# First routed scores issued among the last local tile's steps, with each bank and room waited for at its first use

## The chip, the cores and the metric

One core of a Trainium2 chip. The metric is the device time of one execution in microseconds (us), median of several. TensorE is called PE, VectorE DVE, ScalarE ACT, GpSimd POOL; SP is the engine whose queue issues most DMAs.

## The reference

All tensors are fp32; x is 2 sequences of 1024 tokens, 512 wide.

```
xn  = layernorm(x)
A:  q,k,v = xn Wq+bq, xn Wk+bk, xn Wv+bv      (16 query heads, 4 key/value heads, 32 wide)
    q,k = rope(rmsnorm(q)), rope(rmsnorm(k))
    local attention: a key is seen when it is not later and at most 64 back
    out_A = attention @ Wo + bo
B:  gate = softmax(xn W_gate) over 16 heads; each token keeps its best head's k (one shared
    key) and its best head's v times the gate (one shared value)
    out_B = causal attention of all 16 heads' q over the shared k and v, full length
x + out_A + out_B
```

## The kernel before

The kernel has two stages. The **local stage** goes in 8 rounds of 256 tokens (two tiles of 128): products with the weights (banks gemm, 2 of them), layernorm and transposes (bank tp1), and for each tile the local attention: scores in four banks (win), maxima on DVE, exponentials on ACT, sums on DVE, scaling on POOL, four transposes p_t through the win banks with a copy on ACT each, values (bank av), a copy and a subtraction (attn, on ACT and DVE), twelve matmuls with Wo (project, in a gemm bank), and a DVE addition into x_res (event res_r). SP then stores these rows to the DRAM tensor `partial` (event res_stored).

The **routed stage** does B in 8 units (4 groups of 4 heads, 2 sequences). A unit u has 48 row_scores (a matmul of queries against all keys in an s_ps bank and a masked maximum on DVE), which give each query's maximum; these are turned (max_in_rows) and written into two more rows of the query operand by two small DMAs (r_row by ACT's queue, r_row_lo by SP's). Then come 36 key_scores (one matmul of 512 columns in an st_ps bank, an exponential of it on ACT into a room p_t, on POOL a causal mask for the diagonal ones and an addition for pairs), key_values and key_sums (bank od_ps), row_done (copy on ACT) and finish (transposes on PE, scaling on DVE). The maxima of unit 0 (first_max) are made during the local stage, so unit 0 has only key_scores on, and in the meantime the row_scores of unit 1 run. PSUM has 8 banks; the routed stage's s_ps (4), st_ps (3) and od_ps are the same banks as gemm, tp1, win and av. Its SBUF rooms lie over tensors of the local stage too: p_t over p_loc, p_loc_t and qkv, the pair sums over cos_t and others, the query operand q_op over the weights w_tok, out_sb[1] over x_res.

The order of all steps is written out by a planner (`make_plan`, class `Routed`) with assumed costs per engine: it emits one list of steps, and every engine's program walks that list in order and issues its own part, with semaphore waits. So a step's place in the list is its place on PE, ACT, DVE, POOL and SP. `Routed.run` takes whichever of finish, row maximum, key scores and values can go first, in that order where they tie.

Between the stages stands one step, `routed_banks`. On PE it waits for the last product's bank to be read, res_r, p_t_r and at_lo of the last tile and r_lo of unit 0. On ACT, which issues nothing else for it, it is

```
lane.wait_ge(*M["gemm_read"].of((ROUNDS - 1, *LAST_UNIT)))
lane.wait_ge(*M["res_stored1"].of(ROUNDS - 1))
lane.wait_ge(*M["res_bias"].of(last_tile))
lane.wait_ge(*M["pv_mm"].of(last_tile))
```

res_stored1 is the landing of the last tile's store to `partial`. The queries of units 0 and 1 are read back from DRAM by q_load steps on SP, each of three DMAs (three blocks of rows); `qt` steps on SP store the queries of the last round, four DMAs each.

Of the kernel before, what the change touches and what calls it, by code (L numbers as in the profile page):

```python
# [38 lines left out]
MAXIMA = [(i, h, c0) for i in range(IT) for c0 in range(0, (i + 1) * P, 512) for h in range(HQ)]  # L39
S_BANKS, ST_BANKS = 4, 3  # L40
ROUTED_SCALE = float(DK) ** -0.5

# [5 lines left out]
for _k, (_i, _j) in enumerate(PRODUCTS):  # L48
    if (_k - _i * (_i + 1) // 2) % 2:
# [15 lines left out]
              ("qt", 1), ("qt", 2), ("qt", 3)]  # L65
LAST_UNIT = UNITS[-1]
LAST_CHUNKS = [(ROUNDS - 1, 2), (ROUNDS - 1, 3)]

# [8 lines left out]

Q_LANDS = 4.0

# [95 lines left out]
def make_plan():  # L175
# [103 lines left out]

    def take_routed(n, kind, a, freed):  # L280
        do("picked", n, kind, a)
        yield 0, [("V", 0.7)], freed
        yield 0, [("V", 1.1)]
        if (n, kind, a) == (ROUNDS - 1, "fv", 1):
            do("routed_rooms")
            p.rooms = True
            for quarter in range(2):
                do("q_load", 0, 0, 0, quarter)
        if kind == "fv":
            do("fv_out", n, a)  # L290
# [23 lines left out]
    def take_qt(n, kind, c, freed):  # L314
        do("qt", n, c)
        yield 0, [("A", 0.4), ("V", 0.45)], freed
        if c == 0 and n < S // PAIR:
            for _ in range(6):
                yield None
            p.q_kept = n  # L320
        if n == ROUNDS - 1 and c:
            u, quarters = ((0, (2, 3)), (1, (0, 1)), (1, (2, 3)))[c - 1]
            for quarter in quarters:
                do("q_load", u, 0, u, quarter)
                p.q_lands[u, quarter] = p.now + Q_LANDS * (1 + quarter % 2)

    def attend(m, a):
# [46 lines left out]
        p.av_free = None  # L374
        p.take("av", ("values", m, a), ("at_lo", (m, a)))
        do("values", m, a)
        yield 1.0, []
        do("attn", m, a)

        def attn_end(end):  # L380
            p.av_free = end + HOP
        yield 0, [("A", 0.6), ("V", 0.7)], attn_end
        yield 0, [("", SLACK)]
        project_out(m, a)
# [63 lines left out]
    p.run(when)  # L448
    do("routed_banks")
    routed_stage(p)  # L450
    return p

# [7 lines left out]
class Routed:  # L460
# [151 lines left out]
    def take_finish(self):  # L612
# [9 lines left out]
        if i == IT - 1:  # L622
            self.do("store", u, hg, b)
            if u + B < UNITS_ROUTED:
                self.do("partial_load", *self.unit(u + B))

    def run(self):
        rows = UNITS_ROUTED * IT
        while self.finished < rows:
            if self.later and self.later[0] <= self.now:  # L630
                self.take_low()
            ways = [(self.next_finish(), self.take_finish), (self.next_maximum(), self.take_maximum),
                    (self.next_scores(), self.take_scores), (self.next_values(), self.take_values)]
# [11 lines left out]
def routed_stage(p):  # L645
    Routed(p).run()

# [45 lines left out]
def mixed_attention_kernel(nc, counts, x, w_tok, w_qt, w_o, b_qkv, b_o, w_norm, scale, rope, ident, mask, rows, rank,  # L693
# [88 lines left out]
    psum1.close()  # L782
    s_ps = [pb(top, f"s_ps{n}", [P, 512]) for n in range(S_BANKS)]
    st_ps = [pb(top, f"st_ps{n}", [P, HQ, P]) for n in range(ST_BANKS)]
# [30 lines left out]
    out_sb = [Room(t).piece(IT, P) for t in (q_t, x_res)]  # L815
    p_t = [room.piece(HQ, P) for room in [Room(t) for t in p_loc] for _ in range(3)]
    p_t += [Room(t).piece(HQ, P) for t in (*p_loc_t, *qkv)]
# [10 lines left out]
    def turned_back(u, i):  # L828

        return s_ps[plan.turn["s", ("finish", u, i)]][:, 0:2 * P].rearrange("p (n c) -> p n c", n=2)  # L830

    DST = {"kvg": w_tok_p, "q": w_tok_p, "fk": w_tok_p, "fv": w_tok_p, "qt": w_qt_p, "wo": w_o_p}
    SRC = {"kvg": w_tok, "q": w_tok, "fk": w_tok, "fv": w_tok, "qt": w_qt, "wo": w_o}
    last_tile = (ROUNDS - 1, 1)

    def qt_of(part, n, c):

        if (n, c) in LAST_CHUNKS:
            rooms = [t[:, :, :].rearrange("p h d -> p (h d)") for t in (rope_b, rope_sq)]
            return rooms[c % 2][:, part * PAIR:(part + 1) * PAIR].bitcast(F32R)  # L840
        return qt[part][:, c % 2, :]

    def stored(n, c):
# [20 lines left out]
    def tensor_program(e):  # L864
        lane = Lane(e)
        for step, *key in plan.steps:
# [142 lines left out]

            elif step == "routed_banks":  # L1010
                lane.wait_ge(*M["gemm_read"].of((ROUNDS - 1, *LAST_UNIT)))
                lane.wait_ge(*M["res_r"].of(last_tile))
                lane.wait_ge(*M["p_t_r"].of((*last_tile, QUADS - 1)))
                lane.wait_ge(*M["at_lo"].of(last_tile))
                lane.wait_ge(*M["r_lo"].of(0))

            elif step == "row_scores":
                u, hg, b, t = key
                i, h, c0 = MAXIMA[t]
                lane.wait_ge(*M[f"q_in{b}{i // 2}"].of(hg))  # L1020
                bank = plan.turn["s", ("row_scores", u, t)]
                if free := freed(("s", bank), ("row_scores", u, t)):
                    lane.wait_ge(*free)
                cols = max(min((i + 1) * P - c0, 512), 2 * P)
# [4 lines left out]
            elif step == "max_in_rows":  # L1029
# [5 lines left out]
                else:  # L1035
                    lane.wait_ge(*M["rs_max"].of((u, len(MAXIMA) - 1)))
                    if free := freed(("s", plan.turn["s", ("max_in_rows", u)]), ("max_in_rows", u)):
                        lane.wait_ge(*free)
                e.nop(nofuse=True)
# [4 lines left out]
            elif step == "key_scores":  # L1044
# [5 lines left out]
                if u == 0:  # L1050
                    lane.wait_ge(*M[f"q_in0{i // 2}"].of(0))
                if k >= ST_BANKS:
                    lane.wait_ge(*M["rp_exp"].of((u, k - ST_BANKS)))
                elif u:
                    lane.wait_ge(*M["rp_exp"].of((u - 1, len(PRODUCTS) - ST_BANKS + k)))
                e.matmul(st_ps[k % ST_BANKS][:, :, :], k_stack[0:HALVES + 2, b * S + j * P:b * S + (j + 1) * P],  # L1056
                         q_op[b][0:HALVES + 2, i, :, :], start=True, stop=True).then_inc(
                             *M["rst_mm"].did((u, k)))

            elif step == "key_values":  # L1060
                u, b, k = key
                i, j = PRODUCTS[k]
                if i == j:
                    lane.wait_ge(*M["rp_diag"].of((u, i)))
                    if i or u:
                        lane.wait_ge(*M["ro_r"].of((u, i - 1) if i else (u - 1, IT - 1)))
                else:
                    lane.wait_ge(*M["rp_exp"].of((u, k)))
# [19 lines left out]
            elif step == "finish":  # L1088
                u, hg, b, i = key
                lane.wait_ge(*M["ro_r"].of((u, i)))  # L1090
                if free := freed(("s", plan.turn["s", ("finish", u, i)]), ("finish", u, i)):
                    lane.wait_ge(*free)
                for h in range(2):
# [5 lines left out]
    def vector_program(e):  # L1099
# [3 lines left out]
        for step, *key in plan.steps:  # L1103
# [218 lines left out]
            elif step == "finish":  # L1322
# [4 lines left out]
                if i == 0 and hg:  # L1327
                    lane.wait_ge(*M[f"stored{b}"].of(hg - 1))
                if i or u:
                    lane.wait_ge(*M["ro_norm"].of((u, i - 1) if i else (u - 1, IT - 1)))  # L1330
# [14 lines left out]
    def scalar_program(e):  # L1345
# [12 lines left out]
        for step, *key in plan.steps:  # L1358
# [135 lines left out]

            elif step == "routed_banks":
                lane.wait_ge(*M["gemm_read"].of((ROUNDS - 1, *LAST_UNIT)))
                lane.wait_ge(*M["res_stored1"].of(ROUNDS - 1))
                lane.wait_ge(*M["res_bias"].of(last_tile))
                lane.wait_ge(*M["pv_mm"].of(last_tile))
# [32 lines left out]
    def gpsimd_program(e):  # L1532
# [6 lines left out]
        for step, *key in plan.steps:  # L1539
# [98 lines left out]
            elif step == "key_scores":  # L1638
# [9 lines left out]
                elif k in PAIR_OF and SUMMER[u] == "G":  # L1648
# [21 lines left out]
    def sync_program(e):  # L1670
        lane = Lane(e)
        for step, *key in plan.steps:
# [97 lines left out]
            elif step == "q_load":  # L1770
# [8 lines left out]
                else:  # L1779
# [3 lines left out]
                    lane.wait_ge(*M["rst_mm"].of((u - 2, PRODUCTS.index((2 * c + 1, 2 * c)))))  # L1783
                e.nop(nofuse=True)
                for blk, part in ((0, 0), (1, 1), (2, 0)):
                    src = q_parts[part, :, b * IT + 2 * c:b * IT + 2 * c + 2, hg * HQ:(hg + 1) * HQ, :]
                    e.dma_start(q_op[b][blk * DK:(blk + 1) * DK, 2 * c:2 * c + 2, :, :].bitcast(F32), src).then_inc(
                                    *M[f"q_in{b}{c}"].did(hg, inc=16))
# [89 lines left out]
```

## Time and profile before

| | |
|---|---|
| median of 3 executions | 690.85 us (689.47 to 693.93) |
| profiled execution: time, span | 692.62 us, 691.4 us |
| granted clock, mean over the span | 0.982 |
| PE, PE weight loads, DVE, ACT, POOL busy in the span | 94%, 74%, 72%, 52%, 64% |
| last product of the local stage ends, first routed matmul starts | 398.81 us, 399.59 us |

The profile is of one execution; its time is 1.2 us more than its span, and 1.8 us above the median. A busy share says how long an engine had an instruction in work, not that it set the pace. The granted clock is 1.00 at 2.4 GHz and 0.50 at 1.2 GHz.

### The profile page before, as it was taken

The page shows a single profiled execution, that of the slowest core. Times are in us where ns is not written, and L with a number is a line of the kernel's source. Part 1 is how long each engine was busy: PE and PEld are TensorE (multiplying, and loading weights), DVE is VectorE, ACT ScalarE, POOL GpSimd, SP SyncE. Part 2 cuts the span into 40 slices and gives each one's busy share as a digit, 9 for nine tenths or more (in the row PEclk, how much of TensorE's full clock was granted, in tenths as well). Part 3 has the DMA queues.
Part 4 walks back from the last instruction along what each step waited for, and adds up shares of the span by engine and source line. Part 5 has one row for each costly group of instructions (what it writes and reads, how often), then busy time and mean ns, then how long its engine had stood idle before and what let it go on. Part 6 is the DMA issues. An engine that isn't in the chain of part 4 may idle for free.

```text
span 691.4 us, 19466 instructions
## 1 busy us (share of the span) xinstructions
PE 648.9 (94%) x7432; PEld 513.0 (74%) x7432; DVE 497.0 (72%) x1328; ACT 362.3 (52%) x906; POOL 442.5 (64%) x368
## 2 busy tenths in 40 slices
PE   4698999999999899999899789999999999999997
PEld 3577788888788788887788557777767777777775
DVE  3956967677777776697575268887887787879444
ACT  5446444553437244354526345556665665656674
POOL 3965774937393743785395247686868777778740
PEclk9879999999999999999999989999999999999999
DMA  8523213231131122212211742141314131412011
GB/s 302 193 58 102 66 50 100 85 103 54 55 108 58 49 91 73 86 46 66 77 47 51 196 136 70 50 109 49 109 50 109 33 105 49 109 28 85 5 32 34
DMA packets 65134, 56.63 MB, mean 82 GB/s; under 512 B 6672, under 2 KB 49040, under 8 KB 65040
## 3 DMA queue, kind: packets, MB, share of 16 engines
q1 hardware_dynamic: 62896, 54.45, 26.7%
q8 instruction: 59, 0.97, 0.6%
q10 hardware_dynamic: 2144, 0.93, 0.5%
q14 instruction: 35, 0.29, 0.1%
HBM read 37.20 MB, written 17.89 MB: 80 GB/s over the span
## 4 chain that ended last, share of the span: by engine, by line
PE 77%; DVE 9%; POOL 4%; ACT 3%; issue 3%; DMA 2%; ACTq 1%; DVEq 0%; POOLq 0%
PE gemm L908 16%; PE s_ps L1025 11%; PE od_ps L1070 11%; PE st_ps L1056 10%; PE gemm L994 6%; PE od_ps L1084 5%; PE win L968 3%; PE gemm L904 3%; PE win L953 2%; PE s_ps L1094 2%; PE av L980 2%; DMA rope_t<-rope 2%; DVE l_sum L1241 2%; ACT p_loc L1463 2%; DVE l_max L1232 1%
## 5 line engine op out<-in xcount | busy, mean ns | idle before, releaser
L908 PE MATMUL gemm<-w_tok,xt 128*128 128x512 f32 (+1 forms) x768 | 185.9, 384 | 4.5 <-DVE g_exp L1155 2.0
L908 PEld LDWEIGHTS gemm<-w_tok,xt 128*128 128x128 f32 x768 | 131.7, 193 | 29.0 <-DVE g_exp L1155 3.0
L1293 DVE CUSTOM_DVE_ANT_0 s_ps<-s_ps,x_ln 128x512 f32<-128x512 f32 (+3 forms) x224 | 127.6, 619 | 31.1 <-PE s_ps L1025 30.5
L1025 PE MATMUL s_ps<-k_stack,w_tok 96*128 96x512 f32 (+2 forms) x336 | 103.4, 389 | 0.9 <-DVE x_res L1258 0.8
L1056 PE MATMUL st_ps<-w_tok,k_stack 98*128 98x512 f32 x288 | 100.5, 416 | 2.7 <-ACT p_loc L1509 2.7
L1509 ACT ACTIVATE p_loc<-st_ps 128x512 f32<-128x512 f32 x144 | 77.4, 599 | 41.2 <-PE st_ps L1056 31.6
L1603 POOL TENSOR_TENSOR rope_b<-qkv,sin_t 128x128 f32<-128x128 f32 (+1 forms) x32 | 27.5, 879 | 79.4 <-DVE qkv L1207 79.3
L1025 PEld LDWEIGHTS s_ps<-k_stack,w_tok 96*128 96x128 f32 x336 | 56.2, 191 | 28.4 <-DVE picked_fk L1293 10.9
L1463 ACT ACTIVATE p_loc<-win,l_max 128x96 f32<-128x96 f32 x256 | 60.9, 391 | 19.1 <-DVE l_max L1232 19.1
L1509 ACT ACTIVATE p_loc_t<-st_ps 128x512 f32<-128x512 f32 x96 | 52.4, 599 | 20.5 <-PE st_ps L1056 20.0
L904 PE MATMUL gemm<-xt,w_qt 128*128 128x256 f32 x384 | 57.4, 294 | 5.4 <-DVE picked_fv L1186 3.3
L1627 POOL TENSOR_TENSOR p_loc<-p_loc,l_rec 128x1536 f32<-128x1536 f32 x16 | 44.1, 2757 | 26.9 <-DVE l_rec L1244 26.9
L1293 DVE CUSTOM_DVE_ANT_0 s_ps<-s_ps,x_ln,picked_fk 128x128 f32<-128x128 f32 (+3 forms) x112 | 56.8, 554 | 6.0 <-PE s_ps L1025 5.5
L1579 POOL TENSOR_TENSOR rms_y<-rms_v,minus_half 128x20 f32<-128x20 f32 x16 | 58.6, 3664 | 3.3 <-DVE rms_v L1217 2.8
L1056 PEld LDWEIGHTS st_ps<-w_tok,k_stack 98*128 98x128 f32 x288 | 51.3, 192 | 11.8 <-issue 4.4
L994 PE MATMUL gemm<-w_o,attn_t 128*128 128x512 f32 x192 | 54.7, 413 | 3.8 <-DVE attn_t L1249 3.1
L904 PEld LDWEIGHTS gemm<-xt,w_qt 128*128 128x128 f32 x384 | 50.9, 195 | 9.3 <-DVE picked_fv L1186 4.2
L1293 DVE DVE_READ_ACCUMULATOR2_ANT picked_fk<- 128x1 f32 x336 | 47.4, 141 | 0.0
L1645 POOL TENSOR_SCALAR_AFFINE_SELECT p_loc<-p_loc 128x512 f32<-128x512 f32 x40 | 25.0, 634 | 32.7 <-ACT p_loc L1509 32.6
L1472 ACT ACTIVATE p_loc_t<-win 96x512 f32<-96x512 f32 x64 | 36.7, 635 | 16.5 <-PE win L968 16.4
L1070 PE MATMUL od_ps<-p_loc,v_all 128*32 128x128 f32 x1152 | 44.6, 278 | 0.0
L994 PEld LDWEIGHTS gemm<-w_o,attn_t 128*128 128x128 f32 x192 | 34.1, 193 | 10.5 <-issue 3.7
(172 smaller groups left out, 1298.6 us busy)
## 6 DMA issues: line engine op xcount, KB each, us to landing
w_tok<-q_parts SPq DMA_DIRECT2D x96, 128.0 KB, 2.7
q_parts<-qt SPq DMA_DIRECT2D x120, 64.0 KB
x_ln<-x SPq DMA_DIRECT2D x8, 512.0 KB, 4.5
x_res<-x SPq DMA_DIRECT2D x16, 256.0 KB, 2.8
partial<-x_res SPq DMA_DIRECT2D x16, 256.0 KB, 2.7
w_tok<-partial SPq DMA_DIRECT2D x8, 512.0 KB, 5.3
raw<-w_tok SPq DMA_DIRECT2D x3, 1024.0 KB, 12.5
v_win<-v_rows SPq DMA_DIRECT2D x64, 48.0 KB, 2.2
```

Source lines behind the costliest of these rows:

```text
L904: i = e.matmul(g[:, 0:PAIR], w_qt_p[r][:, k, a * P:(a + 1) * P], xs[l][:, k, :], start=first, stop=last)
L908: i = e.matmul(g[:, 0:cols], xs[l][:, k, a * P:(a + 1) * P], w_tok_p[r][:, k, c0:c0 + cols], start=first, stop=last)
L994: i = e.matmul(gemm[bank][:, :], attn_t[l][:, kc, :], w_o_p[r][:, kc, :], start=kc == 0 and q == 0, stop=kc == KC - 1 and q == 2)
L1025: e.matmul(s_ps[bank][:, 0:cols], q_op[b][0:HALVES, i, h, :], k_stack[0:HALVES, b * S + c0:b * S + c0 + cols], start=True, stop=True).then ...
L1056: e.matmul(st_ps[k % ST_BANKS][:, :, :], k_stack[0:HALVES + 2, b * S + j * P:b * S + (j + 1) * P], q_op[b][0:HALVES + 2, i, :, :], start=T ...
L1070: mm = e.matmul(od_ps[h * DK:(h + 1) * DK, 0, :], v_all[:, b * IT + j, 0:DK], p_t[k % RING][:, h, :], start=i == j, stop=ends_row(k))
L1293: e.tensor_tensor_reduce(out=s[:, 0:cols], in0=s[:, 0:cols], in1=causal[:, S - width + c0:S - width + c0 + cols], scale=1.0, scalar=dst if ...
L1463: i = e.activation(p_loc[a][:, g, quad, :], win[:, g, quad * KEYS:(quad + 1) * KEYS], ACT.Exp, bias=l_max[:, a, n:n + 1])
L1472: e.activation(p_loc_t[quad][0:KEYS, :, :].rearrange("p g q -> p (g q)"), win[0:KEYS, quad, :], ACT.Copy).then_inc(*M["p_t_r"].did((m, a, ...
L1509: e.activation(p_t[k % RING][:, :, :], st_ps[k % ST_BANKS][:, :, :], ACT.Exp, scale=ROUTED_SCALE).then_inc(*M["rp_exp"].did((u, k)))
L1579: e.tensor_tensor(rms_y[:, :], rms_v[:, :], minus_half[:, :].to_broadcast([P, NH]), ALU.pow).then_inc(*M["rms_r"].did((n, a)))
L1627: e.tensor_tensor(p_l, p_l, l_rec[:, a, :].unsqueeze(2).to_broadcast([P, H, KEYS]), ALU.mult).then_inc(*M["p_r"].did((m, a)))
```

## The change

`routed_banks` is gone. The last tile's values and attn steps take the first four key_scores of unit 0 with them (two ahead of values, two behind attn), all ahead of the last project on every engine. Each wait of `routed_banks` is put where the bank or room is first used. The s_ps banks are numbered the other way round, so that banks 0 and 1 of the order are a win bank and tp1, and banks 2 and 3 the gemm banks. The wait for the store to `partial` moves to DVE's first finish of unit 1, where out_sb[1] is first written. The q_loads of units 0 and 1 move four tiles in a step instead of two, so 4 steps of three DMAs instead of 8, and stand earlier in the list: unit 0's ahead of the step `picked` of the last fv product, unit 1's behind the qt chunks 1 and 2 rather than 2 and 3.

```
+EARLY_SCORES = (2, 2)
-Q_LANDS = 4.0
+Q_LANDS = 6.0
     def take_routed(n, kind, a, freed):
+        if (n, kind, a) == (ROUNDS - 1, "fv", 1):
+            for quarter in (0, 2):
+                do("q_load", 0, 0, 0, quarter)
...
-            for quarter in range(2):
-                do("q_load", 0, 0, 0, quarter)
...
-        if n == ROUNDS - 1 and c:
-            u, quarters = ((0, (2, 3)), (1, (0, 1)), (1, (2, 3)))[c - 1]
-            for quarter in quarters:
-                do("q_load", u, 0, u, quarter)
-                p.q_lands[u, quarter] = p.now + Q_LANDS * (1 + quarter % 2)
+        if n == ROUNDS - 1 and c in (1, 2):
+            quarter = 2 * (c - 1)
+            do("q_load", 1, 0, 1, quarter)
+            p.q_lands.update({(1, quarter + q): p.now + Q_LANDS for q in range(2)})
...
+        if (m, a) == LAST_TILE:
+            p.routed = Routed(p)
+            p.routed.scores_at(p.now, EARLY_SCORES[0])
         do("values", m, a)
         yield 1.0, []
         do("attn", m, a)
...
+        if (m, a) == LAST_TILE:
+            p.routed.scores_at(p.now, EARLY_SCORES[1])
         yield 0, [("", SLACK)]
         project_out(m, a)
...
-    do("routed_banks")
-    routed_stage(p)
+    p.routed.run()
...
+    def scores_at(self, now, count):
+        self.now = now
+        for _ in range(count):
+            self.take_scores()
+        self.p.now = self.now
     def run(self):
+        self.now = self.p.now
+        self.s_free = [max(free, self.now) for free in self.s_free]
...
-    s_ps = [pb(top, f"s_ps{n}", [P, 512]) for n in range(S_BANKS)]
+    s_ps = [pb(top, f"s_ps{n}", [P, 512]) for n in range(S_BANKS)][::-1]
...
+    def scores_bank_free(bank, step):
+        if free := freed(("s", bank), step):
+            return free
+        if bank == 0:
+            return M["p_t_r"].of((*last_tile, 0))
+        if bank == 1:
+            return M["r_lo"].of(0)
+        return M["res_r"].of(last_tile)
...  PE, key_scores:
+                else:
+                    lane.wait_ge(*M["p_t_r"].of((*last_tile, k + 1)))
...  PE, key_values of the first row:
+                    else:
+                        lane.wait_ge(*M["at_lo"].of(last_tile))
...  DVE, finish:
+                elif i == 0 and b:
+                    for a in range(2):
+                        lane.wait_ge(*M[f"res_stored{a}"].of(ROUNDS - 1))
...  ACT:
-            elif step == "routed_banks":
...
             elif step == "key_scores":
                 lane.wait_ge(*M["rst_mm"].of((u, k)))
+                if u == 0 and k < RING:
+                    if k < 2 * RING_P_LOC:
+                        lane.wait_ge(*M["p_t_r"].of((*last_tile, QUADS - 1)))
+                    elif k < 2 * RING_P_LOC + QUADS:
+                        lane.wait_ge(*M["pv_mm"].of(last_tile))
+                    else:
+                        lane.wait_ge(*M["gemm_read"].of((ROUNDS - 1, *LAST_UNIT)))
...  POOL, first pair sums:
+                    else:
+                        lane.wait_ge(*M["res_bias"].of(last_tile))
...  SP, q_load:
+                i0, i1 = 2 * c, 2 * c + (2 if u >= B else PART)
                 for blk, part in ((0, 0), (1, 1), (2, 0)):
-                    src = q_parts[part, :, b * IT + 2 * c:b * IT + 2 * c + 2, ...]
+                    src = q_parts[part, :, b * IT + i0:b * IT + i1, ...]
```

## Rows read from the trace of the kernel before

**Rows 1.** The page: busy time of PE; granted clock in 40 equal slices.

```profile
PE 648.9 (94%) x7432; PEld 513.0 (74%) x7432; DVE 497.0 (72%) x1328; ACT 362.3 (52%) x906; POOL 442.5 (64%) x368
...
PEclk9879999999999999999999989999999999999999
```

**Rows 2.** Windows (PE, weight loads, DVE, ACT, POOL busy; clock; DMA): the routed stage.

```profile
410.00:650.00 240.00, 239.38 (x3608) 176.53 (x3607) 197.26 (x759) 145.58 (x296) 181.64 (x170) 1.00 0.25 69
650.00:691.00 41.00, 36.22 (x699) 26.36 (x699) 17.20 (x41) 27.43 (x56) 13.65 (x16) 0.99 0.10 29
```

**Rows 3.** Chain of waits between the stages (start, us, what).

```profile
394.30 0.61 ACT attn_t L1480
...
395.77 3.05 PE gemm L994 x12
398.84 0.70 DVE x_res L1258
399.56 3.75 DMA partial<-x_res
...
403.38 0.60 ACT p_loc L1509
```

**Rows 4.** Timeline of PE over the same stretch, with idle time before an instruction and its releaser.

```profile
391.88 0.60 PE L968 MATMUL win<-idt,p_loc 128*96 128x128 f32 x4
393.16 1.08 PE L980 MATMUL av<-p_loc_t,v_win 96*32 96x128 f32 x32 [0.68 <-ACT p_loc_t L1472]
395.77 3.04 PE L994 MATMUL gemm<-w_o,attn_t 128*128 128x512 f32 x12 [1.53 <-DVE attn_t L1249]
399.59 0.74 PE L1025 MATMUL s_ps<-k_stack,w_tok 96*128 96x256 f32 x4 [0.78 <-DVE x_res L1258]
400.17 0.63 PE L1056 MATMUL st_ps<-w_tok,k_stack 98*128 98x512 f32 x2
...
404.12 0.76 PE L1056 MATMUL st_ps<-w_tok,k_stack 98*128 98x512 f32 x1 [2.43 <-ACT p_loc L1509]
```

**Rows 5.** Timeline of ACT and of POOL around the first exponentials.

```profile
392.51 0.59 ACT L1472 ACTIVATE p_loc_t<-win 96x512 f32<-96x512 f32 x1 [0.54 <-PE win L968]
403.38 2.14 ACT L1509 ACTIVATE p_loc<-st_ps 128x512 f32<-128x512 f32 x4 [8.48 <-DMA partial<-x_res]
404.11 1.22 POOL L1645 TENSOR_SCALAR_AFFINE_SELECT p_loc<-p_loc 128x512 f32<-128x512 f32 x2 [15.97 <-ACT p_loc L1509]
```

**Rows 6.** Windows: clock around the two idle stretches of PE.

```profile
384.00:386.00 2.00, 0.47 (x10) 0.30 (x2) 0.77 (x2) 0.60 (x1) 1.84 (x1) 1.00 1.08 246
386.00:388.00 2.00, 1.65 (x8) 1.19 (x7) 0.00 (x0) 0.00 (x0) 2.00 (x2) 0.67 0.74 164
...
403.80:410.60 6.80, 6.48 (x30) 4.86 (x31) 4.01 (x13) 3.82 (x8) 4.35 (x5) 0.50 0.30 91
```

**Rows 7.** Chain of waits, the same operations at either clock.

```profile
408.03 1.58 PE s_ps L1025 x3
409.61 0.43 PE st_ps L1056
...
412.06 0.89 PE s_ps L1025 x3
412.95 0.46 PE st_ps L1056 x2
```

**Rows 8.** Timeline of SP: its DMA issues from the last round's stores on.

```profile
371.16 2.22 SPq L1703 DMA_DIRECT2D q_parts<-qt  x4
...
385.32 0.60 SPq L1759 DMA_DIRECT2D w_tok<-w_tok  x1
386.04 2.29 SPq L1703 DMA_DIRECT2D q_parts<-rope_b  x4
...
391.63 5.78 SPq L1787 DMA_DIRECT2D w_tok<-q_parts  x12
397.45 2.43 SPq L1751 DMA_DIRECT2D partial<-x_res  x3
```

More of the change, by code:

```diff
@@ L40 @@
 S_BANKS, ST_BANKS = 4, 3
+RING_P_LOC = 3
 ROUTED_SCALE = float(DK) ** -0.5
@@ L66 @@
 LAST_UNIT = UNITS[-1]
+LAST_TILE = (ROUNDS - 1, 1)
+EARLY_SCORES = (2, 2)
 LAST_CHUNKS = [(ROUNDS - 1, 2), (ROUNDS - 1, 3)]
@@ L642, in run @@
         self.p.now = self.now
-def routed_stage(p):
-    Routed(p).run()
 class Mark:
@@ L815, in mixed_attention_kernel @@
     out_sb = [Room(t).piece(IT, P) for t in (q_t, x_res)]
-    p_t = [room.piece(HQ, P) for room in [Room(t) for t in p_loc] for _ in range(3)]
+    p_t = [room.piece(HQ, P) for room in [Room(t) for t in p_loc] for _ in range(RING_P_LOC)]
     p_t += [Room(t).piece(HQ, P) for t in (*p_loc_t, *qkv)]
@@ L830, in turned_back @@
         return s_ps[plan.turn["s", ("finish", u, i)]][:, 0:2 * P].rearrange("p (n c) -> p n c", n=2)
+    def scores_bank_free(bank, step):
[6 more added lines that the diff above has]
+        return M["res_r"].of(last_tile)
     DST = {"kvg": w_tok_p, "q": w_tok_p, "fk": w_tok_p, "fv": w_tok_p, "qt": w_qt_p, "wo": w_o_p}
     SRC = {"kvg": w_tok, "q": w_tok, "fk": w_tok, "fv": w_tok, "qt": w_qt, "wo": w_o}
-    last_tile = (ROUNDS - 1, 1)
+    last_tile = LAST_TILE
     def qt_of(part, n, c):
@@ L841, in qt_of, with queries @@
         return qt[part][:, c % 2, :]
+    def queries(u, i):
+        return M[f"q_in{u % B}{i // 2 if u >= B else i // PART * 2}"].of(u // B)
     def stored(n, c):
@@ L1008, in tensor_program @@
                          stop=True).then_inc(*M["first_mm"].did(t))
-            elif step == "routed_banks":
[L1011 to L1015, printed above, removed]
             elif step == "row_scores":
@@ L1019, in tensor_program @@
                 i, h, c0 = MAXIMA[t]
-                lane.wait_ge(*M[f"q_in{b}{i // 2}"].of(hg))
+                lane.wait_ge(*queries(u, i))
                 bank = plan.turn["s", ("row_scores", u, t)]
-                if free := freed(("s", bank), ("row_scores", u, t)):
-                    lane.wait_ge(*free)
+                lane.wait_ge(*scores_bank_free(bank, ("row_scores", u, t)))
                 cols = max(min((i + 1) * P - c0, 512), 2 * P)
@@ L1036, in tensor_program @@
                     lane.wait_ge(*M["rs_max"].of((u, len(MAXIMA) - 1)))
-                    if free := freed(("s", plan.turn["s", ("max_in_rows", u)]), ("max_in_rows", u)):
-                        lane.wait_ge(*free)
+                    lane.wait_ge(*scores_bank_free(plan.turn["s", ("max_in_rows", u)], ("max_in_rows", u)))
                 e.nop(nofuse=True)
@@ L1050, in tensor_program @@
                 if u == 0:
-                    lane.wait_ge(*M[f"q_in0{i // 2}"].of(0))
+                    lane.wait_ge(*queries(u, i))
                 if k >= ST_BANKS:
@@ L1090, in tensor_program @@
                 lane.wait_ge(*M["ro_r"].of((u, i)))
-                if free := freed(("s", plan.turn["s", ("finish", u, i)]), ("finish", u, i)):
-                    lane.wait_ge(*free)
+                lane.wait_ge(*scores_bank_free(plan.turn["s", ("finish", u, i)], ("finish", u, i)))
                 for h in range(2):
@@ L1493, in scalar_program @@
                 e.dma_start(row_of(b, 0), hi.bitcast(F32)).then_inc(*M["r_row"].did(u, inc=16))
[L1495 to L1499, printed above, removed]
             elif step == "key_scores":
@@ L1784, in sync_program @@
                 e.nop(nofuse=True)
+                i0, i1 = 2 * c, 2 * c + (2 if u >= B else PART)
                 for blk, part in ((0, 0), (1, 1), (2, 0)):
-                    src = q_parts[part, :, b * IT + 2 * c:b * IT + 2 * c + 2, hg * HQ:(hg + 1) * HQ, :]
-                    e.dma_start(q_op[b][blk * DK:(blk + 1) * DK, 2 * c:2 * c + 2, :, :].bitcast(F32), src).then_inc(
+                    src = q_parts[part, :, b * IT + i0:b * IT + i1, hg * HQ:(hg + 1) * HQ, :]
+                    e.dma_start(q_op[b][blk * DK:(blk + 1) * DK, i0:i1, :, :].bitcast(F32), src).then_inc(
                                     *M[f"q_in{b}{c}"].did(hg, inc=16))
```

## The prediction

> **What bounds the kernel now.** I read the page first: PE is busy in 94% of the span and its clock is full except at the start and in two slices in the middle [rows 1]. Then the windows: from 410 to 650 us PE is busy 239.38 of 240 us at clock 1.00, with DVE at 197.26 [rows 2]. The reader should see that in the routed stage nobody but PE sets the pace, so whatever starts that stage earlier, with the same work left, ends the kernel earlier. PE's idle time is small there (0.62 us in 240) and 4.78 us in the last 41, in the last unit, which the change does not touch by name. So the change is worth what it takes out of PE's time between the stages. There I read the chain of waits and PE's timeline. The last tile's transposes end at 392.48; then PE idles 0.68 us for ACT's copy, runs the values, idles 1.53 us for ACT's and DVE's copies, runs the project, idles 0.78 us for the addition into x_res, runs eight row_scores and three key_scores, and idles 2.43 us [rows 3, 4]. The last wait is for ACT's first exponential: ACT had nothing to do for 8.48 us, until the store to `partial` landed at 403.31, 3.75 us after SP issued it [rows 3, 5]. The exponentials themselves needed nothing of that store. Right behind this hole PE's clock is 0.50 from 403.8 to 410.6, while PE is busy 6.48 of 6.80 us [rows 6].
>
> **The change part by part.**
>
> *The store's wait leaves ACT.* ACT can take exponentials as soon as PE has made scores. The fourth key score needs the first one's bank, so PE's 2.43 us hole [rows 4] is this wait and nothing else: minus 2.43 us. What is late next? The other waits of the removed step are over early: the last qt bank long before (its DRAM store is issued from 388.4 or sooner), the values by 394.24, the POOL addition into x_res before 404.11 by 15.97 us [rows 4, 5, 8]. The new place of the wait is DVE's first finish of unit 1. It comes after unit 0's whole work, over 30 us behind the landing, so it costs nothing; without that cover DVE would be held, and the row maxima and finishes queued behind it with PE after them, one for one.
>
> *Four key_scores go ahead of the project.* On PE: the first two stand between the last p_t and the values. Their banks are the win banks whose copies precede the last one, so they can go at 392.48, and two take 0.46 us [rows 7], inside the 0.68 us hole. The next two stand behind the values, in the 1.53 us hole; the bank of the one is free with the last copy, of the other with the first exponential, which is over by 393.8. All four are then missing behind the project: four times 0.23 is minus 0.92 us [rows 7]. If the holes did not hide them the term would be 0. On ACT: two exponentials come between the last p_t copy, which ends at 393.10, and the attn copy, which starts at 394.30. Four of them take 2.14 us, so 0.51 apart [rows 3, 5]; two end at about 394.2 to 394.3, just when the values are done. I take 0.1 us of delay; the bounds are 0 and 0.6 (one exponential), and the project, DVE's addition and everything after are what would be delayed. The other two run while DVE subtracts and PE projects. On POOL: two masks, a pair sum and another mask, beside nothing, since POOL is idle for 15.97 us there [rows 5]. DVE has no part in a key score of unit 0. On SP: the third key score takes with it a q_load of unit 2, whose three DMAs now stand ahead of the last store to `partial`, and that store is queued behind its waits: the third key score's matmul and the landings of the last qt stores. The first is over at about 394.8 and three issues take about 1.4 us (12 in 5.78), so SP is free by 396.5, three us ahead of the addition that the store waits for [rows 3, 8]. Cost nothing.
>
> *Banks waited for at first use.* Behind the project two row_scores, in the win bank and in tp1, go at once at 398.82; the third needs a gemm bank and res_r, at 399.54 [rows 3]. Four row_scores take from 399.59 to 400.17, 0.145 each, so 0.29 us of work comes into the 0.78 us hole and 0.49 of the hole stays [rows 4]: minus 0.29. It could be 0 (if only the first bank's order matters) or 0.78.
>
> *Queries loaded by halves.* SP was never idle from 371 to 397: it works through stores and 24 DMAs of q_load, each issue 0.48 us [rows 8]. Halved, they cost some 5.8 us less. Unit 0's now come when the last fv product has ended, ahead of SP's first qt store, in time in which SP has nothing to issue, so they push nothing: the stores, v_in and res_load of the last tile behind them keep their times. The row r_row_lo of unit 0 was issued at 385.32 behind all of unit 0's loads [rows 8]; it now comes some 4 us sooner, which the early key_scores need (they wait for it at 392.5). Unit 1's second half is issued before 390 instead of up to 397.4. PE waited for none of these before, so the gain is 0, and 0 to the store's time as well: at 397.45 SP issued the two older stores only because it got there then [rows 8]. The Trainium skill speaks against this edit: Perfetto Trace Analysis, section DMA Optimizations, says that splitting transfers into smaller ones can let some work start sooner, and here they are made larger. By that rule the first key and row scores would wait for twice the bytes; no hole of PE before was for these loads, and both first halves are issued more than 5 us ahead of use, so the sum would be the same unless that lead were used up. The changed landing estimate of the planner (6.0 for 4.0) concerns loads that in its own time are over before the routed stage starts, so it changes no order.
>
> *The clock.* At 0.50 three 512-column row_scores take 1.58 us and one key score 0.43; at full clock 0.89 and 0.23 [rows 7]. The stretch at half clock has 6.48 us of PE work, so at most half, 3.24 us, comes back [rows 6]; with the row_scores (1.58 against 0.89, a bit less than half) I take 3.0. The condition is that the clock does not fall. Before both falls PE had done little: 0.47 us in the 2 us from 384 [rows 6], and in the 4.5 from 399.59 only 2.1, up to the hole of 2.43 [rows 4]. Between 392 and 400, where holes of 0.68, 1.53 and 0.78 us stand between the work, it did not fall. In the new kernel these holes are smaller, about 0.2, 1.06 and 0.49, and none follows. The Trainium skill (Perfetto Trace Analysis, section Matmul Optimizations) says that PE's clock follows how much it is used, so that matmuls should come back to back; the trace agrees, with 0.50 right behind the 2.43 us hole, and by the rule too this term goes with the hole.
>
> *The order written anew.* The planner starts the routed stage with four key scores done, so the list differs from there on. Nothing in the trace shows the new list. Below, PE has 0.62 us of idle to give in 240 [rows 2] and little of the last unit's 4.78; above, a worse order could cost a hole of the size seen between the stages, 1 to 2.4 us [rows 4]. I take 0, as PE's row of 410 to 650 shows the planner leaving nearly nothing in seven units.
>
> **Sum.** 2.43 + 0.92 + 0.29 + 3.0 - 0.1 = 6.54 us. Against the profiled execution's own time, 692.62, this is 686.08 us. How does this stand to the median of 690.85? The term that need not be in every execution is the clock: without it the profiled execution would have been 689.6, which is just the lowest of the three runs, 689.47. So I take the sum as an absolute time, 686.0, and not 6.54 off the median: the gain against the median is then 4.9 us, 0.7%.
>
> **The rivals.**
>
> *The clock does fall again around 400, or later.* For it: it fell twice in 20 us, and holes of 1.06 and 0.49 us stay. Against it: it held through larger ones. A fall half as long as the second costs about 1.5 us, one as long 3.0, on top of the forecast. Time: 687.6 to 689.1.
>
> *The gain is larger against the median.* If the median had this half clock as the profiled execution did, its 1.8 us less come from elsewhere, and the whole 6.54 comes off it: 684.3, and with 0.6 us from the newly written order 683.7.
>
> *The change doesn't do what it says: the early key_scores do not fit their holes.* If the two exponentials ahead of attn cost their full 0.6 us and the two ahead of the values are late by as much, 1.1 us of the gain goes: 687.2. The order of waits speaks for it, the 1.2 us between ACT's copies [rows 5 and 3] against it.
>
> *Slower: PE comes to wait for DVE in every unit.* DVE is at 82% from 410 to 650 [rows 2], and during the hole and the half clock it could catch up with unit 1's maxima (4.01 busy of 6.80 us [rows 6]). The planner counts 0.618 us for a 512-column maximum. With PE at full speed and four key scores fewer to put between, PE would stand at banks that DVE has not read. It decides from about 1 us for each of the seven units that have maxima: there the whole gain is gone. At 2 us a unit the time is 686.0 + 14 = 700. Against it: 42.7 us of DVE's time is free in these 240, and PE waited in none of them for longer than the 0.62 us in all.
>
> **How the numbers follow.** About 1%, 6.9 us, is what a measurement of this kernel can tell from no change. Forecast (684.8 to 687.0, centre 686.0): 0.45. Clock falls again: 0.17. Larger against the median, under 684.8: 0.24, most of it just about the border of 683.94. Early scores don't fit (687.0 to 688): 0.08. Slower: 0.06. Of the forecast's own spread little lies beyond 1%. Faster by over 1%: 0.22; within 1%: 0.73; slower by over 1%: 0.05. The range leaves out what lies beyond the full sum off the median with one us more, 682.9, and above the clock case with the half us of a late exponential, 689.6.
>
> **What the changed profile would show.** Right: two key_scores on PE between the last p_t and the values and two behind them; ACT's first exponential at about 393 and no wait of ACT for `partial`; the attn copy still right behind the values; after the project a hole of about 0.5 us that ends with the x_res addition, behind two row_scores; no PE hole over 0.5 us in the ten us after; clock 1.00 from 400 to 410; unit 1's maxima turned 6 to 7 us sooner than before. Wrong: a clock of 0.50 there, an attn copy over 0.3 us late, PE idle of over 2 us in the long window, or a project that starts late because the first key scores waited for r_row_lo or for the first queries.

## The result and the profile after

The changed kernel takes 685.26 us (four executions, 685.13 to 685.68); the kernel before, now with four executions, 692.39 us (689.47 to 694.76). The ratio is 0.9899, 95% interval 0.9869 to 0.9929: 7.1 us less, 1.0%. The profiled execution took 685.68 us, its span 684.4 us, against 692.62 and 691.4.

First PE's timeline between the stages (the stretch of [rows 4]; L998 is the last p_t, L1080 key_scores, L1010 the values, L1024 the project, L1047 row_scores):

```profile
392.78 0.71 PE L1080 MATMUL st_ps<-w_tok,k_stack 98*128 98x512 f32 x2
393.71 1.08 PE L1010 MATMUL av<-p_loc_t,v_win 96*32 96x128 f32 x32 [0.22 <-ACT p_loc_t L1501]
394.72 0.73 PE L1080 MATMUL st_ps<-w_tok,k_stack 98*128 98x512 f32 x2
396.32 3.04 PE L1024 MATMUL gemm<-w_o,attn_t 128*128 128x512 f32 x12 [0.87 <-DVE attn_t L1274]
399.21 0.40 PE L1080 MATMUL st_ps<-w_tok,k_stack 98*128 98x512 f32 x1
399.44 0.40 PE L1047 MATMUL s_ps<-k_stack,w_tok 96*128 96x256 f32 x2
400.15 0.51 PE L1047 MATMUL s_ps<-k_stack,w_tok 96*128 96x256 f32 x2 [0.31 <-DVE x_res L1283]
```

The holes of 0.68, 1.53, 0.78 and 2.43 us have become 0.22, 0.87, 0.31 and none. (The local stage ran 0.55 us late in this execution, so all times stand that much higher than before.) ACT's timeline shows what took the place of its 8.48 us of waiting [rows 5]:

```profile
393.06 0.59 ACT L1501 ACTIVATE p_loc_t<-win 96x512 f32<-96x512 f32 x1 [0.53 <-PE win L998]
393.75 1.08 ACT L1540 ACTIVATE p_loc<-st_ps 128x512 f32<-128x512 f32 x2
394.86 0.60 ACT L1509 ACTIVATE attn_t<-av 128x512 fp32r<-128x512 f32 x1
395.35 1.08 ACT L1540 ACTIVATE p_loc<-st_ps 128x512 f32<-128x512 f32 x2
399.64 0.60 ACT L1540 ACTIVATE p_loc<-st_ps 128x512 f32<-128x512 f32 x1 [3.21 <-PE st_ps L1080]
```

Two exponentials fit exactly between the last copy and attn: the values end at 394.83 by the chain of waits (393.71 and 1.12), attn's copy starts at 394.86. From the start of the values to the start of the project it is 2.61 us in both kernels, so the early scores delayed nothing on this way. The chain there, and SP's timeline (beside [rows 3] and [rows 8]):

```profile
393.71 1.12 PE av L1010 x32
394.83 0.02 issue
394.86 0.61 ACT attn_t L1509
...
399.40 0.70 DVE x_res L1283
400.11 0.04 issue
400.15 0.51 PE s_ps L1047 x2
```

```profile
367.34 2.71 SPq L1821 DMA_DIRECT2D w_tok<-q_parts  x6
371.61 2.23 SPq L1736 DMA_DIRECT2D q_parts<-qt  x4
...
381.58 0.61 SPq L1792 DMA_DIRECT2D w_tok<-w_tok  x1
...
400.12 0.34 SPq L1784 DMA_DIRECT2D partial<-x_res  x1
402.21 0.38 SPq L1832 DMA_DIRECT2D w_tok<-partial  x1
```

SP waits with its load from `partial` for the landing of the store, so the store issued at 400.12 had landed by 402.21, 2.1 us later and not 3.75. Nobody waits for it now but SP. The windows (beside [rows 2] and [rows 6]; PE, weight loads, DVE, ACT, POOL busy, clock, DMA):

```profile
386.00:388.00 2.00, 1.50 (x6) 1.03 (x7) 0.00 (x0) 0.00 (x0) 2.00 (x2) 0.84 0.30 85
388.00:390.00 2.00, 2.00 (x8) 1.56 (x7) 0.00 (x0) 0.59 (x1) 0.61 (x1) 0.50 0.29 86
...
404.00:406.00 2.00, 2.00 (x23) 1.20 (x25) 1.97 (x9) 2.00 (x5) 1.59 (x3) 1.00 0.95 280
...
410.00:650.00 240.00, 239.46 (x3658) 176.13 (x3656) 194.23 (x749) 145.70 (x296) 180.61 (x169) 1.00 0.25 68
```

The clock stays 1.00 where it was 0.50; the earlier fall, near 387, is still there.

**A yardstick that leaves the local stage out.** Executions differ by some us before either kernel has reached the change: of two kernels below that are the kernel before up to there, one starts its last project at 394.63 us (e1), the other at 397.88 (e2), against 395.77. What makes them differ was not settled. The granted clock from 20 to 40 us differs too, 0.71 in the profiled execution before and 0.81 after, but it does not explain this: it was 1.00 in e3, whose last project starts late, at 397.46. So beside each median I give the time from the start of the last project to the end of the span. Before it is 691.4 - 395.77 = 295.63 us, after 684.4 - 396.32 = 288.08: 7.55 us less. Windows over just these stretches:

```profile
395.77:691.40 295.63, 286.61 (x4355) 210.89 (x4355) 221.31 (x826) 176.73 (x359) 199.64 (x190) 0.99 0.25 69
```

```profile
396.32:684.40 288.08, 282.20 (x4351) 207.56 (x4351) 220.65 (x826) 174.91 (x356) 198.16 (x188) 1.00 0.24 66
```

PE is idle 3.14 us less: 2.43 for the last hole, 0.47 for the one behind the project, 0.24 spread over the rest. It is busy 4.41 us less: 0.92 is the four key scores that now stand ahead of the project, and the half clock's 6.48 us of work at double speed is up to 3.24; 0.25 stays unassigned.

### The profile page after: what moved, and what is told of

Its sections match the earlier page's. It is cut to its first block, busy times and chain, and to the rows that moved or that the text cites. A ratio compares the mean times of both kernels' runs of the same rounds, so it can differ in the third digit from the quotient of the medians.

```text
span 684.4 us, 19451 instructions
## 1 busy us (share of the span) xinstructions
PE 646.0 (94%) x7432; PEld 510.2 (75%) x7432; DVE 496.3 (73%) x1328; ACT 362.5 (53%) x906; POOL 442.6 (65%) x368
## 4 chain that ended last, share of the span: by engine, by line
PE 78%; DVE 9%; POOL 4%; ACT 3%; issue 2%; DMA 2%; ACTq 1%; DVEq 0%; POOLq 0%
PE gemm L938 17%; PE s_ps L1047 12%; PE od_ps L1096 11%; PE st_ps L1080 10%; PE gemm L1024 6%; PE od_ps L1110 5%; PE win L998 3%; PE gemm L934 3%; PE win L983 2%; PE s_ps L1119 2%; DMA rope_t<-rope 2%; PE av L1010 2%; DVE l_sum L1266 2%; ACT p_loc L1492 2%; DVE l_max L1257 1%
## 5 line engine op out<-in xcount | busy, mean ns | idle before, releaser
L1047 PE MATMUL s_ps<-k_stack,w_tok 96*128 96x512 f32 (+2 forms) x336 | 101.5, 385 | 0.3 <-DVE x_res L1283 0.3
L1080 PE MATMUL st_ps<-w_tok,k_stack 98*128 98x512 f32 x288 | 99.0, 413 | 0.2 <-ACT p_loc L1540 0.2
L1047 PEld LDWEIGHTS s_ps<-k_stack,w_tok 96*128 96x128 f32 x336 | 55.0, 188 | 28.3 <-DVE picked_fk L1318 12.4
L1024 PE MATMUL gemm<-w_o,attn_t 128*128 128x512 f32 x192 | 54.8, 414 | 3.2 <-DVE attn_t L1274 2.4
L1080 PEld LDWEIGHTS st_ps<-w_tok,k_stack 98*128 98x128 f32 x288 | 50.5, 189 | 9.0 <-ACT p_loc L1540 2.1
L1024 PEld LDWEIGHTS gemm<-w_o,attn_t 128*128 128x128 f32 x192 | 34.1, 193 | 10.0 <-issue 3.2
```

The lines of the kernel that those rows point to most:

```text
L1024: i = e.matmul(gemm[bank][:, :], attn_t[l][:, kc, :], w_o_p[r][:, kc, :], start=kc == 0 and q == 0, stop=kc == KC - 1 and q == 2)
L1047: e.matmul(s_ps[bank][:, 0:cols], q_op[b][0:HALVES, i, h, :], k_stack[0:HALVES, b * S + c0:b * S + c0 + cols], start=True, stop=True).then ...
```

## The experiments

Eleven runs. In this table "rest" is the time from the start of the last project to the end of the span, in the profiled execution: one value for each kernel. The changed kernel, profiled twice, differs by 0.15 us from itself, so differences of that size are not read.

| run | median us (executions) | ratio to before, 95% | rest us |
|---|---|---|---|
| before | 692.39 (4); 692.97 (17), 692.67 (11) and 692.92 (17) beside the runs | | 295.63 |
| changed kernel | 685.26 (4) | 0.9899 (0.9869 to 0.9929) | 288.08 |
| a1_changed_again | 685.17 (6) | 0.9890 (0.9866 to 0.9914) | 287.93 |
| e1_wait_only | 687.05 (5) | 0.9911 (0.9875 to 0.9947) | 290.37 |
| e8_loads_only | 688.00 (12) | 0.9946 (0.9924 to 0.9969) | 290.80 |
| e2_fill_hole | 689.73 (10) | 0.9946 (0.9926 to 0.9966) | 292.92 |
| e3_no_early | 687.76 (7) | 0.9905 (0.9876 to 0.9933) | 289.44 |
| e4_small_loads | 686.78 (4) | 0.9896 (0.9854 to 0.9938) | 288.04 |
| e5_store_wait_kept | 688.44 (6) | 0.9932 (0.9911 to 0.9953) | 291.18 |
| e6_fill_first | 682.44 (5) | 0.9856 (0.9833 to 0.9880) | 288.09 |
| e7_more_early | 686.26 (6) | 0.9908 (0.9886 to 0.9931) | 288.82 |
| e9_early_two | 685.32 (6) | 0.9910 (0.9876 to 0.9944) | 288.08 |
| e10_fill_early | 683.92 (6) | 0.9887 (0.9853 to 0.9921) | 288.06 |

**The wait alone** (before, with two edits):

```
 ACT, routed_banks:
-                lane.wait_ge(*M["res_stored1"].of(ROUNDS - 1))
 DVE, finish:
+                elif i == 0 and b:
+                    for a in range(2):
+                        lane.wait_ge(*M[f"res_stored{a}"].of(ROUNDS - 1))
```

> The kernel before with one edit: ACT no longer waits for the last residual store; DVE's first finish of unit 1 waits for it instead. Theory (the 2.43 us hole of PE and the half clock behind it are that wait): the hole goes and the clock stays 1.00 from 400 to 410, so of the change's 7 us some 5.5 come with this one line, time about 686.8; the holes of 1.53 and 0.78 us ahead stay. Rival (the early key scores are what matters, and without them ACT or the clock falls behind anyway): the time stays within 2 us of the kernel before.

Measured: 687.05 us, the rest 5.26 us shorter. The hole is gone with the clock's fall, and the holes ahead stay (windows 398 to 410: PE busy 11.55 of 12, clock 1.00):

```profile
394.63 3.04 PE L994 MATMUL gemm<-w_o,attn_t 128*128 128x512 f32 x12 [1.54 <-DVE attn_t L1249]
398.45 0.74 PE L1025 MATMUL s_ps<-k_stack,w_tok 96*128 96x256 f32 x4 [0.78 <-DVE x_res L1258]
```

```profile
398.00:410.00 12.00, 11.55 (x121) 8.26 (x122) 10.89 (x44) 7.50 (x15) 8.39 (x10) 1.00 0.60 182
```

One line carries 5.26 of the 7.55 us. The rival is out.

**The clock alone** (before, ahead of key score 3 of unit 0; adds matmuls that nobody reads):

```
+                if (u, k) == (0, 3):
+                    for _ in range(9):
+                        e.matmul(od_ps[:, :, :], k_stack[0:HALVES, 0:P], q_op[0][0:HALVES, 2, :, :], start=True,
+                                 stop=True)
```

> The kernel before with nine extra matmuls of 512 columns on PE, whose results nobody reads, in the hole in front of the fourth key score; every wait as before. They need 9 x 0.23 = 2.1 of the 2.43 us. Theory (idleness of PE lowers the clock, worth 3.0 to 3.2 us in the profiled execution): the hole stays in the time, the clock stays 1.00 behind it, and the time falls to about 689.4, with a smaller spread between executions. Rival (the clock fell for another reason, or the matmuls at half clock were hidden beside DVE): the clock is 0.50 there all the same, or the time stays at the median of before, about 692.

```profile
403.64 2.23 PE L1055 MATMUL od_ps<-w_tok,k_stack 96*128 96x512 f32 x9
406.34 0.50 PE L1061 MATMUL st_ps<-w_tok,k_stack 98*128 98x512 f32 x1 [0.47 <-ACT p_loc L1514]
```

```profile
403.80:410.60 6.80, 6.33 (x42) 4.27 (x40) 4.63 (x19) 4.19 (x9) 3.89 (x5) 1.00 0.52 157
```

Measured: 689.73 us, 3.2 us under its neighbours' 692.97; the rest is 2.71 us shorter. The key score behind the hole waits for ACT as before, only the clock is another. The wait was the same and the time was not: the clock's term is shown by itself, at 2.7 to 3.2 us. The spread is 4.3 us over ten executions (687.74 to 692.03) and 7.0 over the seventeen of before beside them; whether it shrank, as expected, these numbers are too few to say.

**No early scores** (`EARLY_SCORES = (0, 0)`).

> The changed kernel with EARLY_SCORES (0, 0), so no key score goes ahead of the project. Theory (four key scores in holes are worth 0.92 us, the rest comes from the waits): 685.26 plus 0.9, about 686.2; clock full. Rival (the early scores keep PE's clock up through the holes of 1.5 and 0.8 us): the clock falls around 400 and the time is 687.7 to 689.

Measured: the rest is 1.36 us longer than the changed kernel's; PE is busy in it for 283.13 us instead of 282.20, which is the four scores, and idle 0.43 us longer, 0.38 of that between 410 and 650; why was not traced. The clock stayed 1.00 from 398 to 410, behind the hole of 1.53 us that is left ahead of the project, so the rival is out in the profiled execution. The median, 687.76, lies where the rival put it all the same. The profiled execution was late already at its last project (397.46), but it is also the slowest of the seven, so it does not say where the others lost their time; that stays open.

**Small loads in the changed kernel** (the q_load steps, their places and marks as before).

> The changed kernel with the query loads of units 0 and 1 as before: eight steps of two tiles at their old places. Theory (no PE hole was for these loads, all land ahead of use): within 0.3 us of the changed kernel, 685.3. Rival (SP's queue would hold the row of minima or the first queries back until the early key scores are due, or the residual store): PE waits ahead of the last values or the clock falls, 687 or more.

Measured: rest 288.04 against 288.08. Within the change the loads are worth nothing. With the loads as before the last store, issued at 401.45, landed only when SP went on at 406.27, 4.8 us later instead of 2.1, and nobody but SP waited for it. The median is 1.5 us above the changed kernel's, of executions between 685.3 and 687.17; a1's lie between 683.6 and 687.28, so medians of four to six do not tell 1.5 us apart here.

**The changed kernel again.**

> The changed kernel once more, as the yardstick of its chip for the three kernels run beside it. Both theories: ratio to the kernel before 0.990, within 0.3% of the first comparison.

Measured as expected, 0.9890.

**The store's wait put back** (changed kernel, ACT):

```
+                if (u, k) == (0, sum(EARLY_SCORES)):
+                    lane.wait_ge(*M["res_stored1"].of(ROUNDS - 1))
```

> The changed kernel with ACT's wait for the last residual store put back, at the first exponential behind the four early ones (key score 4). Theory (the wait, not the missing early scores, made the hole): ACT stands from 399.6 until the store lands at 402.2; PE has key scores 4 to 6 and six row scores to issue and then idles for about 1 us, and about 1 us of the gain is lost, 686.3, 2.5 to 3 if the clock falls behind the hole. Rival (four early key scores and the quieter SP queue make the wait harmless): within 0.3 us of the changed kernel.

```profile
402.67 0.50 PE L1080 MATMUL st_ps<-w_tok,k_stack 98*128 98x512 f32 x1 [1.51 <-ACT p_loc L1542]
```

```profile
403.40:407.90 4.50, 4.50 (x28) 3.56 (x29) 3.74 (x15) 2.86 (x7) 3.43 (x4) 0.62 0.49 144
```

Measured: 688.44 us, 3.3 above a1; the rest is 3.25 longer. The hole is 1.51 us and the clock falls behind it, to 0.50 between 404.5 and 407.5. With everything else of the change in place, this wait costs close to half of the gain.

**The loads alone** (before, with the change's q_load steps, places, marks and Q_LANDS, and all waits of routed_banks).

> The kernel before with the change's query loads alone (four steps of four tiles, earlier); every wait of routed_banks kept. In the run with the store's wait put back the store landed 2.1 us after its issue, against 3.75 before. Theory (fewer loads in flight let the last store land sooner, ACT is released sooner): the hole of 2.43 us shrinks to about 0.8, 1.6 us are won, and up to 3 more in executions in which the clock now holds; ratio 0.994 to 0.998. Rival (loads are worth nothing, as the blind prediction had it): the hole stays 2.4 us and the ratio is 1.000.

```profile
399.47 2.00 DMA partial<-x_res
401.46 0.03 ACTq L678
401.49 0.04 issue
401.53 0.60 ACT p_loc L1512
```

```profile
402.18 0.50 PE L1059 MATMUL st_ps<-w_tok,k_stack 98*128 98x512 f32 x1 [0.58 <-ACT p_loc L1512]
402.52 0.34 PE L1028 MATMUL s_ps<-k_stack,w_tok 96*128 96x384 f32 x1
```

This is the chain of waits and PE's timeline. The store lands in 2.00 us, the hole is 0.58 us instead of 2.43, and the clock is 1.00 from 402 to 410. What the DMA engines did from 395 to 405 us, in 40 slices of 0.25 us (busy share in tenths, and GB/s), before:

```profile
DMA  9999999999999999999999997222119798982034
GB/s 295 254 262 230 270 271 254 221 262 246 270 230 279 197 230 246 279 254 352 410 377 369 385 385 287 107 107 106 74 49 172 270 320 295 221 270 58 23 115 147
```

and in e8:

```profile
DMA  9984222100000000000008980000038988961293
GB/s 369 401 295 148 107 107 82 57 25 0 0 0 0 0 0 0 0 0 0 0 0 319 401 328 0 0 0 0 0 41 213 311 213 279 254 221 49 78 274 94
```

In e8 the engines stand all but still from 397.25 us until the store, issued at 399.47, moves its 256 KB in three slices from 400.25. Before, they are busy without a break when the store is issued at 399.56, and stay so to 401.25. The loads are not all that stands ahead of it: SP issued the two older stores only from 397.45 on, behind the twelve loads, and in e8 the first of them already at 391.37. The rate from 399.5 to 401, 352 to 410 GB/s, is that of the lone store in e8 and not the 197 to 295 of the time of the loads, so by these rates (an estimate) most of what was in front of the last store then were the two older stores, which the loads had held back. No run separates the two. The rest is 4.83 us shorter, the median 4.9. So moving the wait and moving the loads are two ways to the same 5 us, and do not add: once ACT does not wait for the store, its landing matters to nobody (e4).

**Filling the first hole** (changed kernel, PE, ahead of the project of tile (7, 0); adds matmuls that nobody reads):

```
+                    if (m, a) == (ROUNDS - 1, 0):
+                        lane.wait_ge(*M["r_lo"].of(0))
+                        lane.wait_ge(*queries(0, 0))
+                        for _ in range(6):
+                            e.matmul(tp1[:, :, :], k_stack[0:HALVES, 0:P], q_op[0][0:HALVES, 0, :, :], start=True,
+                                     stop=True)
```

> The changed kernel with six extra matmuls of 512 columns, results unread, into tp1 in the 1.5 us hole ahead of the project of tile (7, 0), near 384.7, where both kernels' clock falls for 3.4 us afterwards. Theory (an idle PE lowers the clock): the clock stays 1.00 from 386 to 392, the transposes and project chunks there run at full speed, and 1.5 us are won against the changed kernel, 683.8; the kernel beats both. Rival (ACT's copies and POOL set the pace there, or six matmuls are too few): the time stays within 0.4 us of the changed kernel.

```profile
386.00:388.00 2.00, 2.00 (x14) 1.71 (x13) 0.00 (x0) 1.00 (x2) 0.96 (x1) 1.00 0.29 86
388.00:390.00 2.00, 2.00 (x15) 1.57 (x12) 0.59 (x1) 0.94 (x3) 0.00 (x0) 1.00 0.39 100
```

Measured: 682.44 us, 2.7 under a1 beside it and the fastest of all. The clock stays 1.00. From the start of the project of tile (7, 0) to the end of the span it is 681.2 - 384.41 = 296.79 us against 684.2 - 386.03 = 298.17 in a1's profile: 1.4 us, against 1.5 expected; the rest of the 2.7 lies ahead of the place where the edit stands.

**More steps ahead of the last project.** e7 takes a third key score and two row_scores there and tells the planner that banks 2 and 3 come free 0.8 us later:

```
+EARLY_SCORES = (2, 3)
+            for _ in range(2):
+                p.routed.take_maximum()
+            p.now = p.routed.now
 run:
+        self.now = self.p.now - 0.8
+        self.s_free = [max(free, self.now if bank < 2 else self.p.now) for bank, free in enumerate(self.s_free)]
```

> The changed kernel with a third key score and the first two row scores (banks 0 and 1) ahead of the last project, and with the planner told that banks 2 and 3 come free 0.8 us behind it. Theory (what is left are holes of 0.87 and 0.31 us on PE, and only they can be filled): 0.5 to 0.6 us won, 684.7. Rival (the row maxima on DVE delay the addition into x_res, or the newly written order costs as much): no gain or a loss of up to 0.5 us.

```profile
396.18 3.02 PE L1027 MATMUL gemm<-w_o,attn_t 128*128 128x512 f32 x12 [0.40 <-DVE attn_t L1277]
...
435.25 0.41 PE L1122 MATMUL s_ps<-idt,rope_b 128*128 128x128 f32 x2 [0.29 <-DVE picked_fk L1321]
436.47 0.47 PE L1083 MATMUL st_ps<-w_tok,k_stack 98*128 98x512 f32 x1 [0.81 <-DMA w_tok<-w_tok]
```

The holes between the stages are filled as meant (0.40, and none behind the project), and the rest is 0.74 us longer all the same. In the new order all 36 of unit 0's key scores stand ahead of the turning of unit 1's maxima; behind it PE has too little to do until the row is written, and waits 0.81 us for its DMA. e9 forces two key scores behind the project (`self.scores_at(self.p.now - 0.8, 2)`, and all banks free 0.3 us behind these), which leaves one behind the turning.

> The changed kernel with a third key score and two row scores ahead of the last project, as in the run before this, but with two key scores forced right behind the project and the planner's times otherwise as in the change, so that 35 and not 36 of unit 0's key scores stand ahead of the turning of unit 1's maxima. Theory (the run before lost its 0.5 us to PE waiting 0.8 us at 436 for the row that was written late, not to the early steps themselves): holes of 0.4 and 0 between the stages, no wait over 0.3 us near 436, and 0.3 to 0.6 us less than the changed kernel from the last project's start to the end (288.1). Rival (any key score taken early is missing later as cover): again a wait near 436, and no gain.

Measured: no such wait any more (PE's longest near there is 0.2 us), but the rest is 288.08, the changed kernel's to the hundredth, and the median 685.32. The three steps ahead of the project are 0.52 us of work, and the hole of 0.31 us behind it is filled too. But PE's idle time in the rest is 6.02 us instead of 5.88, with 0.97 from 410 to 650 instead of 0.54, and it is busy only 0.14 us less (282.06 instead of 282.20). Where the other 0.38 of busy time came from was not traced. Both theory and rival had part of it: the late row was e7's loss, and still nothing was gained.

**Both together** (e9 with e6's six unread matmuls at e6's place).

> The same, with the six unread matmuls of the fastest kernel so far in the hole near 384. Theory (both effects add): 682.0, the fastest of all. Rival: 682.4 to 683, as that kernel without the early steps.

Measured: 683.92 us, above the theory's 682.0 and the rival's 682.4 to 683. From the start of the project of tile (7, 0) to the end it is 682.3 - 385.52 = 296.78 us, against 682.6 - 384.41 = 298.19 in e9: the filled hole's 1.4 us once more. That is e6's 296.79 too, so the early steps add nothing to it.

## Why the prediction was right, point by point

The time, 686.0 forecast and 685.26 measured, was within a microsecond; the sum of its terms, 6.54, stands against 7.55 in the profiles. The 1.01 between them are 0.18 at the banks, 0.24 at the clock (if it gave all of its 3.24), 0.1 of delay that did not come, 0.24 of idle time elsewhere and 0.25 unassigned. By its steps:

**The store's wait, 2.43.** Right, and shown by e1 and e5: with the wait there is a hole, without it none. How large the hole is, the store's landing says (e8).

**Four key scores, 0.92.** Right as a count of work; they stand in the holes as forecast, and e3 loses 1.36 without them. The 0.1 us of delay did not come: the attn copy starts 1.15 us behind the start of the values, and 1.14 before.

**Banks at first use, 0.29.** Mis-sized: 0.47. The planner put a key score beside the two row scores, and the hole is 0.31 and not 0.49.

**Queries by halves, 0.** Right inside the change (e4), wrong as it was argued. I wrote that the loads give "0 to the store's time as well", since SP issued the store at once. The issue of the last store was not late, but its landing was: twelve loads issued from 391.63 on and the two older stores behind them [rows 8] kept the DMA engines busy, and the store took 3.75 us [rows 3] instead of 2.0. Alone the loads are worth 4.83 us (e8). I looked at SP's queue and not at the DMA engines behind it. The Trainium skill, DMA: Bandwidth & Descriptors, section Latency and other measured facts, says that the fixed cost of a transfer is smaller when the memory is lightly loaded. The trace agrees in direction only, with 2.0 to 2.1 us for the same store once the engines are free: it does not part a smaller fixed cost from the time that the engines spent on others' data, busy as they were before for 1.7 us behind the store's issue.

**The clock, 3.0.** Right: 2.71 and 3.2 in e2, at most 3.24 by the profile. The section of the Trainium skill that the prediction names speaks of power that follows use; that it is the clock is what the rows show.

**The order written anew, 0.** Right for this kernel, and less certain than it was put: e7 lost some 1.3 us against what its filled holes promised. The rival that ended slower had named a neighbour of it, PE standing behind DVE's maxima; what came was PE standing behind the row's DMA.

**How the sum stands to the median.** This step failed. I took the lowest of three runs, 689.47, for an execution without the half clock, and the sum for an absolute time that is 4.9 us under the median. The fourth execution moved the median to 692.39, and it is 692.67 to 692.97 in the longer series: the profiled execution, half clock and all, was an ordinary one, and the gain is 7.1 us. e2 shows the same: filling the hole takes 3.2 us off the median, nearly all that the half clock can cost. Whether the execution of 689.47 was without it, no profile shows. So the premise of the rival "the gain is larger against the median", which was given 0.24, was the right one. Its time, 684.3, did not come, as the median of three was itself 1.5 to 2.1 us low. That the time came out right is luck in part: the sum was set against the profiled execution, for a reason that did not hold, and that one was typical. The range's lower end, 682.9, is not the sum it names either; 690.85 less 6.54 and one more is 683.3.

What the changed profile was to show came: ACT's first exponential at 393.75, no wait of ACT for the store, clock 1.00 from 400 to 410, and unit 1's maxima turned at 430.9 instead of 437.0.

## What to carry to other kernels

A common gate between two stages lets its slowest wait, here a store that the waiting engine had no use for, hold everything; put each wait at the first use on the engine that uses it, and price the hole with the half clock behind it, which here cost more than the hole. A DMA that is waited for can be made faster by getting other DMAs out of its way, even when its own issue is on time: look at what is in flight as well as at the queue. Two repairs of one wait do not add, so run each alone before either is given the credit.

## What the runs showed of the hardware that I had not expected

Matmuls that nobody reads can pay: six of them (1.4 us of PE time, in a hole of 1.53) kept the clock at 1.00 through the local stage's last 6 us and gave 1.4 us. And the clock fell to 0.50 behind a hole of 1.51 us in e5's profiled execution, while holes of 1.53 and 0.78 us some 4 us apart left it at 1.00 in the profiles of before, e1 and e8; what decides between these was not settled.
